# Six-layer stack on Trainium2: key blocks of values copied from the tile's own buffer in 14 or 16 transfers, instead of by a store and a reload through memory off the chip

## The chip, the cores and the metric

One core of one Trainium2 chip runs the whole program. The metric is device time in microseconds (us), from three timed runs and one profiled execution. Smaller is better.

## The reference

The program computes a network of four pairs of blocks (attention over a context, then a feed-forward block). The change touches only the second half of the third pair, a stack of six local-attention layers over x of 2 x 512 tokens x 128. Cut to what matters:

```python
DIM, DEPTH, HEADS, DIM_HEAD, WINDOW = 128, 6, 16, 64, 32     # INNER = 16 * 64 = 1024

def local_attention(q, k, v):                 # each b, h, n, d
    nw = n // WINDOW
    bq, bk, bv = (t.reshape(b, h, nw, WINDOW, d) for t in (q, k, v))
    def look(t):                              # a window's keys: the window before it, and itself
        p = jnp.pad(t, ((0, 0), (0, 0), (1, 0), (0, 0), (0, 0)))
        return jnp.concatenate([p[:, :, :nw], p[:, :, 1:]], axis=3)
    bk2, bv2 = look(bk), look(bv)
    sim = jnp.einsum('bhwie,bhwje->bhwij', bq, bk2) * 8.0
    sim = jnp.where(mask, -big, sim)
    return jnp.einsum('bhwij,bhwje->bhwie', jax.nn.softmax(sim, -1), bv2)

for i in range(DEPTH):
    x = attn_layer(shift_tokens(x), Wqkv[i], q_scale[i], k_scale[i], Wo[i]) + x
    x = ffn_layer(shift_tokens(x), ln_g[i], ln_b[i], W1[i], b1[i], W2[i], b2[i]) + x
```

Each window of 32 queries mixes 64 values: those of the window before it and its own. `look` is the step whose values are moved here.

## The kernel before

The program is written by hand, engine by engine, with semaphores; nothing schedules it. `Stack` (line 1208 on) cuts the six layers into N = 48 tiles of 128 tokens, four to a unit (one batch element of one layer), two units to a layer. Tile T is number t = T % 4 of its unit. The loops of PE (TensorE), ACT (ScalarE) and DVE (VectorE) run over T and work on several tiles at once: in the pass of T they project tile T + 2, turn queries and keys of T + 1, score and mix T and add T - 1. SyncE runs `sp_shift(T)` for T = 0 to 47 and, behind it, the loads of the next layer's weights: one of three `wqkv` parts after tiles 3, 4 and 5 of a layer (`load_w`), five more transfers after tile 6 (`load_f`).

The path of the values:

- `act_proj`, line 1397: ACT copies tile T's values (128 tokens x 1,024) from PSUM into `v[:, t % 2, :]`, in two halves. There are two such buffers, so tile T takes the one of tile T - 2.
- `sp_shift`, line 1329: SyncE stores the tile's values to `st_v_out`, 512 KB, in memory off the chip, and signals `v_stored`.
- `v_load`, line 1319: it loads them back into `vv` in another order. `vv` holds for each of four windows w of a tile, in four partition ranges of 32 rows, the keys of half e of the heads, h = 1 for the window itself and h = 0 for the one before. Even and odd tiles have their own four places. A tile's loads: 32 x 4 x 512 (h = 1) and 32 x 3 x 512 (h = 0, windows 1 to 3) for each e, and, where t > 0, two of 32 x 512 from the tile before for window 0. For t = 0 window 0 has no window before it, and its place keeps what is masked away.
- `pe_mix`, line 1586: PE multiplies with `vv`, waits for `vshift[t]` and `p_evac`, and signals `pv_done`. `sp_shift(T)` waits for `pv_done` of tile T - 2 before it writes `vv` again.

The lines of the chain's view in this stretch: 1385 projections, 1404 squares, 1420, 1428 and 1433 rotations and sums, 1493 turns of queries and keys, 1514 scores, 1566 turns of probabilities, 1575 their copy `pT`, 1610 turns of the output, 1619 their copy `oT`, 1634 output projection, 1657 and 1670 of the layer norm.

## Time and profile before

| | us |
|---|---|
| median of 3 timed runs | 1956.83 (1955.41 to 1961.53) |
| the profiled execution's own time | 1947.39 |
| its span, first to last instruction | 1945.5 |
| of it the stack, about 563 to 1466 | 903 |

PE is busy in 83% of the span, DVE in 65%, ACT in 50%, POOL in 39%. A busy share is a sum over all stages. What ends a wait in one stage stands in the list of waits (engine and line, what it waited for, total, times, longest) and in the chain, which is followed back from the last instruction. SPq is SyncE's queue: its rows are transfers being issued, and the time from issue to landing stands in the list of DMA issues.

### The profile page before, as it was taken

To read this page: it belongs to the slowest core of one execution; us is meant where nothing else is said; L and a number is where in the kernel's file an instruction comes from. 1 tells how busy PE (TensorE), PEld (TensorE's weight loads), DVE (VectorE), ACT (ScalarE), POOL (GpSimd) and SP (SyncE) were. 2 spreads that over 40 slices of the span, in tenths; PEclk is the share of its full clock that TensorE was granted. 3 is DMA by queue.
4 is the path that set the end of the run, shared out by engine and by line. 5 is a ranking of instruction groups with operands and counts; after the bars stand their busy time and mean duration, and the time that the engine had idled before them with its cause. 6 is when DMAs were issued, how large, how long until landed. Compare 5 with 4: busy or idle time off the path is not lost.

```text
span 1945.5 us, 42200 instructions
## 1 busy us (share of the span) xinstructions
PE 1621.7 (83%) x17249; PEld 1097.3 (56%) x17249; DVE 1255.0 (65%) x2361; ACT 968.0 (50%) x1729; POOL 761.1 (39%) x1082
## 2 busy tenths in 40 slices
PE   3005576999767899989999889999987999999999
PEld 1002254676545666656666656666663677667576
DVE  6847684212866788868888778888853666666311
ACT  1034133332235567656666566666654666666332
POOL 0000020100247666766776657766740333334000
PEclk7556798899888999999999999999998999999999
DMA  3000002010033343433433343343311000000111
GB/s 108 20 4 0 3 1 62 22 33 14 1 113 98 98 117 102 124 81 105 118 103 102 101 102 101 117 109 89 96 35 43 2 1 1 1 2 1 33 33 33
DMA packets 73661, 113.33 MB, mean 58 GB/s; under 512 B 15942, under 2 KB 36012, under 8 KB 73438
## 3 DMA queue, kind: packets, MB, share of 16 engines
q1 hardware_dynamic: 72654, 110.40, 20.6%
q8 instruction: 138, 2.26, 0.5%
q14 instruction: 53, 0.43, 0.1%
q10 hardware_dynamic: 816, 0.24, 0.1%
HBM read 83.95 MB, written 27.50 MB: 57 GB/s over the span
## 4 chain that ended last, share of the span: by engine, by line
PE 60%; DVE 27%; issue 6%; ACT 4%; DVEq 1%; DMA 1%; POOL 0%; ACTq 0%; POOLq 0%; SPq 0%
PE PS L1385 7%; PE PS L1115 6%; PE PS L1106 6%; PE PS L2089 4%; PE PS L2043 3%; PE PS L1634 3%; PE PS L2068 3%; DVE st_t L1428 3%; DVE st_ss L1433 3%; PE PS L1514 2%; DVE st_r L1420 2%; PE PS L1493 2%; PE PS L1586 2%; PE PS L1733 2%; DVE al_hist L459 2%
## 5 line engine op out<-in xcount | busy, mean ns | idle before, releaser
L1462 POOL TENSOR_TENSOR st_r<-st_r,st_t 128x512 f32<-128x512 f32 x192 | 243.6, 1274 | 205.8 <-DVE st_t L1428 205.8
L1385 PE MATMUL PS<-st_wqkv,st_xs 128*128 128x512 f32 x576 | 304.8, 614 | 12.5 <-DVE st_t L1428 8.0
L2174 POOL TENSOR_SCALAR la_p<-la_p,la_rden 128x589 f32<-128x589 f32 x64 | 112.7, 1761 | 245.8 <-DVE la_rden L2193 245.8
L1479 POOL TENSOR_TENSOR st_r<-st_r,st_gy 128x512 f32<-128x512 f32 x192 | 195.1, 1047 | 3.8
L1420 DVE TENSOR_TENSOR st_r<-PS,st_rot 128x512 f32<-128x512 f32 x192 | 129.3, 673 | 99.0 <-ACT st_sqh L1404 98.4
L2187 DVE TENSOR_REDUCE la_nmx<-PS 128x1 f32<-128x589 f32 x128 | 92.7, 766 | 91.8 <-PE PS L2051 91.8
L2149 ACT ACTIVATE la_p<-PS,la_nmx 128x589 f32<-128x589 f32 x128 | 95.0, 747 | 106.6 <-DVE la_nmx L2187 106.6
L1174 ACT ACTIVATE m_h<-PS 128x512 f32<-128x512 f32 x128 | 76.1, 597 | 140.8 <-PE PS L1106 140.8
L1404 ACT ACTIVATE st_sqh<-PS 128x512 f32<-128x512 f32 x192 | 114.4, 596 | 57.4 <-PE PS L1385 56.3
L1199 DVE SCALAR_TENSOR_TENSOR m_y<-PS,m_g,m_y 128x128 f32<-128x128 f32 x112 | 31.5, 345 | 161.0 <-PE PS L1115 161.0
L1428 DVE TENSOR_TENSOR st_t<-PS,st_rot 128x512 f32<-128x512 f32 x192 | 130.6, 680 | 0.0
L1115 PEld LDWEIGHTS PS<-m_w,m_h 128*128 128x128 f32 x1024 | 121.4, 196 | 16.0 <-issue 16.0
L800 POOL MEMSET l_s<- 128x144 f32 x2 | 0.4, 220 | 330.9 <-DVE x L643 216.7
L1433 DVE TENSOR_REDUCE st_ss<-st_sqh 128x8 f32<-128x512 f32 x192 | 129.8, 676 | 0.0
L1493 PEld LDWEIGHTS PS<-cst,st_r 128*128 128x128 f32 x768 | 91.2, 144 | 62.7 <-issue 45.0
L1115 PE MATMUL PS<-m_w,m_h 128*128 128x128 f32 x1024 | 121.7, 279 | 3.0 <-DVE m_y L1201 3.0
L1106 PE MATMUL PS<-xn,m_w 128*128 128x512 f32 x256 | 116.3, 600 | 0.0
L1634 PEld LDWEIGHTS PS<-st_oT,st_wo 128*128 128x128 f32 x768 | 94.7, 200 | 38.0 <-ACT st_oT L1619 29.2
L1493 PE MATMUL PS<-cst,st_r 128*128 128x128 f32 x768 | 111.1, 278 | 4.5 <-POOL st_r L1479 3.7
L1634 PE MATMUL PS<-st_oT,st_wo 128*128 128x128 f32 x768 | 102.9, 289 | 4.8 <-issue 2.7
L1385 PEld LDWEIGHTS PS<-st_wqkv,st_xs 128*128 128x128 f32 x576 | 89.5, 195 | 27.1 <-DVE st_t L1428 16.4
L1514 PEld LDWEIGHTS PS<-st_kT,st_qT 64*32 64x32 f32 x6144 | 64.6, 105 | 62.3 <-issue 62.3
(313 smaller groups left out, 3487.4 us busy)
## 6 DMA issues: line engine op xcount, KB each, us to landing
st_v_out<-st_v SPq DMA_DIRECT2D x48, 512.0 KB, 2.6
st_vv<-st_v_out SPq DMA_DIRECT2D x96, 256.0 KB, 4.2
st_vv<-st_v_out SPq DMA_DIRECT2D x96, 192.0 KB, 4.5
st_wqkv<-in_st_wqkv SPq DMA_DIRECT2D x18, 512.0 KB, 5.7
m_w<-in_m_w SPq DMA_DIRECT2D x32, 256.0 KB, 3.1
st_vv<-st_v_out SPq DMA_DIRECT2D x72, 64.0 KB, 1.9
st_wo<-in_st_wo SPq DMA_DIRECT2D x6, 512.0 KB
st_w<-in_st_w SPq DMA_DIRECT2D x6, 341.0 KB
```

The costliest lines, as they stand in the source:

```text
L1106: pe.matmul(PS[:, c, :], self.w1[:, e % 2, P * c:P * c + P], xn[:, b, :], start=True, stop=True)\
L1115: mm = pe.matmul(PS[:, 4 + u % 2, P * j:P * j + P], self.h[:, u % 2, c, P * j:P * j + P], self.w2[:, e % 2, c, :], start=(c == 0), stop=(c ...
L1385: pe.matmul(PS[:, 2 + m % 2, :], self.xs[:, b, P * t:P * t + P], self.wqkv[:, l % 2, k, 512 * half:512 * half + 512], start=True, stop=Tru ...
L1404: act.activation(self.sqh[:, c % 2, :], ps, ACT.Square).then_inc(self.squares, 1)
L1420: dve.tensor_tensor(h3(self.r[:, t % 2, c, :]), h3(ps), self.rot[:, k, 0, t, :].unsqueeze(1) .broadcast_to([P, 8, D2]), ALU.mult)
L1428: dve.tensor_tensor(h4(self.t2[:, c % 2, :]), turned, self.rot[:, k, 1, t, :] .rearrange("p (s d) -> p s d", s=2).unsqueeze(1).broadcast_t ...
L1433: dve.tensor_reduce(self.ss[:, t % 2, 8 * c:8 * c + 8], h3(self.sqh[:, c % 2, :]), X, ALU.add)\
L1462: pool.tensor_tensor(r, r, self.t2[:, c % 2, :], ALU.add).then_inc(self.added, 1)
L1479: pool.tensor_tensor(r, r, y[:, 8 * c:8 * c + 8].unsqueeze(2).broadcast_to([P, 8, D2]), ALU.mult)\
L1493: mm = pe.transpose(PS[:, 4 + g % 2, P * j:P * j + P], self.r[:, T % 2, g, P * j:P * j + P], ident)
L1634: mm = pe.matmul(PS[:, 7, 0:P], self.wo[:, l % 2, c, :], self.oT[:, c, :], start=(c == 0), stop=(c == 7))
L2174: pool.tensor_scalar(self.p[:, v % 2, 0, :], self.p[:, v % 2, 0, :], self.rden[:, v % 4, 0:1], None, ALU.mult).then_inc(self.scaled0, 1)
```

## The change

`st_v_out`, its store and the wait for it are gone. `v_copy` copies a block of 32 rows x 512 values from `v` straight into its place in `vv`, one transfer for each window w, half e and h: 14 for t = 0 and 16 for the others. The two copies for window 0 from the tile before come first and signal a semaphore of their own, one for even and one for odd tiles (`v_crossed`; the odd one is `al_costs_out`, used earlier in the program and left at 64). The other 14 signal `vshift[t]`. ACT, before it overwrites `v[t % 2]`, waits for the 14 copies of tile T - 2 and the crossed pair of tile T - 1, instead of the store of T - 2. PE waits for the crossed pair too where t > 0.

```diff
-            self.v_out = dram("st_v_out", (4, P, INNER))
...
-        def v_load(self, sp, T, e, h, first, count, to, signal):
+        COSTS_OUT = 64
+        OWN, CROSS = (8 + 6) * 16, 2 * 16
+
+        def v_copy(self, sp, T, e, h, w, signal):
 
+            source = 4 * T + w - (1 - h)
             rows = slice(64 * e + WIN * h, 64 * e + WIN * h + WIN)
-            src = view(self.v_out, ((T % 4) * P + WIN * first) * INNER + 512 * e,
-                       [[INNER, WIN], [WIN * INNER, count], [1, 512]])
-            sp.dma_start(self.vv[rows, to:to + count, e, :], src).then_inc(self.vshift[signal], 16)
+            block = slice(WIN * (source % 4), WIN * (source % 4) + WIN)
+            sp.dma_start(self.vv[rows, 4 * (T % 2) + w, e, :],
+                         self.v[block, source // 4 % 2, 512 * e:512 * e + 512]).then_inc(signal, 16)
+
+        def crossed(self, T):
+
+            odd, units, t = T % 2, T // self.TILES, T % self.TILES
+            count = 2 * units + (t + 1) // 2 if odd else units + t // 2
+            return self.v_crossed[odd], (0, self.COSTS_OUT)[odd] + count * self.CROSS
 
         def sp_shift(self, sp, T):
 
             t = T % self.TILES
-            at = 4 * (T % 2)
-
             sp.wait_ge(self.v_evac, T * 2 + 2)
-            if T >= 4:
-                sp.wait_ge(self.pv_done, T - 3)
-            sp.dma_start(self.v_out[t], self.v[:, t % 2, :]).then_inc(self.v_stored, 16)
-
             if T >= 2:
                 sp.wait_ge(self.pv_done, T - 1)
             if t > 0:
                 for e in range(2):
-                    self.v_load(sp, T - 1, e, 0, 3, 1, at, t)
-            sp.wait_ge(self.v_stored, T * 16 + 16)
+                    self.v_copy(sp, T, e, 0, 0, self.v_crossed[T % 2])
             for e in range(2):
-                self.v_load(sp, T, e, 1, 0, 4, at, t)
-                self.v_load(sp, T, e, 0, 0, 3, at + 1, t)
+                for w in range(4):
+                    self.v_copy(sp, T, e, 1, w, self.vshift[t])
+                    if w:
+                        self.v_copy(sp, T, e, 0, w, self.vshift[t])
...
                 if m == 0 and T >= 2:
 
-                    act.wait_ge(self.v_stored, T * 16 - 16)
+                    act.wait_ge(self.vshift[(T - 2) % self.TILES], ((T - 2) // self.TILES + 1) * self.OWN)
+                    act.wait_ge(*self.crossed(T - 1))
...
             pe.wait_ge(self.p_evac, 2 * T + 2)
-            pe.wait_ge(self.vshift[t], (u + 1) * (64 if t == 0 else 96))
+            pe.wait_ge(self.vshift[t], (u + 1) * self.OWN)
+            if t:
+                pe.wait_ge(*self.crossed(T))
```

SyncE, tile 2 of the first layer, before: `v_out` is the tensor off the chip, `vv` the mixing's buffer.

```order
L1329 DMA st_v_out<-st_v 128x1024 [waits st_v_evac]
L1319 DMA st_vv<-st_v_out 32x512 [waits st_pv_done]
L1319 DMA st_vv<-st_v_out 32x512
L1319 DMA st_vv<-st_v_out 32x4x512 [waits st_v_stored]
L1319 DMA st_vv<-st_v_out 32x3x512
L1319 DMA st_vv<-st_v_out 32x4x512
L1319 DMA st_vv<-st_v_out 32x3x512
```

SyncE, tiles 2 to 4 of the first layer, after, with the weight loads that stand behind tile 3.

```order
L1325 DMA st_vv<-st_v 32x512 [waits st_pv_done,st_v_evac]
L1325 DMA st_vv<-st_v 32x512 x15
L1325 DMA st_vv<-st_v 32x512 [waits st_pv_done,st_v_evac]
L1325 DMA st_vv<-st_v 32x512 x15
L1292 DMA st_qks<-in_st_qks 128x256 [waits st_rot_ready]
L1297 DMA st_wqkv<-in_st_wqkv 128x1024
L1325 DMA st_vv<-st_v 32x512 [waits st_pv_done,st_v_evac]
L1325 DMA st_vv<-st_v 32x512 x13
```

Seven issues with three places to wait became sixteen with one, and the weight loads stand behind a longer row.

ACT, the pass of tile 2, before: the copy into `v` stands between the two copies of `oT`.

```order
L1619 ACTIVATE st_oT<-PS 128x512 [waits st_wo_done,st_o_turned]
L1397 ACTIVATE st_v<-PS 128x512 [waits st_v_stored,st_proj]
L1619 ACTIVATE st_oT<-PS 128x512 [waits st_o_turned]
L1397 ACTIVATE st_v<-PS 128x512 [waits st_proj]
L1549 ACTIVATE st_e<-st_e 128x1024 [waits st_sub_done]
```

The same place after.

```order
L1630 ACTIVATE st_oT<-PS 128x512 [waits st_wo_done,st_o_turned]
L1406 ACTIVATE st_v<-PS 128x512 [waits al_costs_out,st_vshift2,st_proj]
L1630 ACTIVATE st_oT<-PS 128x512 [waits st_o_turned]
L1406 ACTIVATE st_v<-PS 128x512 [waits st_proj]
L1558 ACTIVATE st_e<-st_e 128x1024 [waits st_sub_done]
```

Nothing moved in ACT's row; the first copy into `v` waits for the copies of two tiles in place of one store.

PE, the mixing of tile 2, before.

```order
L1493 MATMUL PS<-cst,st_r 128x128 [waits st_p_evac,st_r_ready]
L1493 MATMUL PS<-cst,st_r 128x128 x3
L1586 MATMUL PS<-st_vv,st_pT 32x128 [waits st_vshift2,st_p_evac]
L1586 MATMUL PS<-st_vv,st_pT 32x128 x31
L1493 MATMUL PS<-cst,st_r 128x128 [waits st_p_evac,st_r_ready]
```

The same place after.

```order
L1502 MATMUL PS<-cst,st_r 128x128 [waits st_p_evac,st_r_ready]
L1502 MATMUL PS<-cst,st_r 128x128 x3
L1597 MATMUL PS<-st_vv,st_pT 32x128 [waits st_v_crossed_even,st_vshift2,st_p_evac]
L1597 MATMUL PS<-st_vv,st_pT 32x128 x31
L1502 MATMUL PS<-cst,st_r 128x128 [waits st_p_evac,st_r_ready]
```

One name more is waited for ahead of the same matmul.

## Rows read from the trace of the kernel before

**Rows 1.** Page, busy time and chain, whole span.
```profile
PE 1621.7 (83%) x17249; PEld 1097.3 (56%) x17249; DVE 1255.0 (65%) x2361; ACT 968.0 (50%) x1729; POOL 761.1 (39%) x1082
...
PE 60%; DVE 27%; issue 6%; ACT 4%; DVEq 1%; DMA 1%; POOL 0%; ACTq 0%; POOLq 0%; SPq 0%
```

**Rows 2.** Stack's stretch: us; busy PE, PEld, DVE, ACT, POOL; PEclk, DMA, GB/s.
```profile
563.00:1466.00 903.00, 830.12 (x12466) 555.00 (x12466) 706.63 (x1092) 570.00 (x931) 597.03 (x985) 0.98 0.37 101
```

**Rows 3.** Waits of SyncE's queue, whole span: total us, times, longest.
```profile
SPq L1329 <- ACT st_v L1397: 376.6, 48, 12.8
...
SPq L1319 <- PE PS L1586: 288.2, 46, 11.5
...
SPq L1336 <- DMA st_v_out<-st_v: 25.0, 11, 2.3
```

**Rows 4.** One line's view: mixing L1586 (idle until), then L1397 (idle until).
```profile
L1586 PE MATMUL PS<-st_vv,st_pT x3072: 272/273/298, 600.3 to 1453.8; 128*32 128x128 f32 x192
...
  issue: 6.7, 40
  ACT st_pT L1575: 2.9, 9
...
  PE PS L1385: 53.7, 53
```

**Rows 5.** Issues, ns min/median/max; then the list of transfers, us to landing.
```profile
L1319 SPq DMA_DIRECT2D st_vv<-st_v_out x264: 303/429/1279, 574.2 to 1424.2; - x132
L1329 SPq DMA_DIRECT2D st_v_out<-st_v x48: 326/338/342, 570.1 to 1413.6; - x48
...
st_vv<-st_v_out SPq DMA_DIRECT2D x96, 192.0 KB, 4.5
...
st_vv<-st_v_out SPq DMA_DIRECT2D x72, 64.0 KB, 1.9
```

**Rows 6.** Timeline (start, us): SyncE's batches, ACT's copies into `v`, one mixing.
```profile
660.98 2.69 SPq L1319 DMA_DIRECT2D st_vv<-st_v_out  x6
...
666.10 0.60 ACT L1397 ACTIVATE st_v<-PS 128x512 f32<-128x512 f32 x1
...
937.08 1.75 SPq L1319 DMA_DIRECT2D st_vv<-st_v_out  x4
...
952.25 2.68 SPq L1319 DMA_DIRECT2D st_vv<-st_v_out  x6
...
957.32 0.60 ACT L1397 ACTIVATE st_v<-PS 128x512 f32<-128x512 f32 x1
...
965.89 1.95 PE L1586 MATMUL PS<-st_vv,st_pT 128*32 128x128 f32 x64
...
967.91 2.84 SPq L1319 DMA_DIRECT2D st_vv<-st_v_out  x6
...
1388.25 3.52 SPq L1319 DMA_DIRECT2D st_vv<-st_v_out  x6
...
1393.32 0.60 ACT L1397 ACTIVATE st_v<-PS 128x512 f32<-128x512 f32 x1
```

**Rows 7.** Timeline, copies with both ends on the chip, and who waited.
```profile
20.08 6.70 SPq L305 DMA_DIRECT2D al_skew<-al_dist  x8
...
27.92 1.63 ACTq L305 DMA_DIRECT2D al_skew<-al_dist  x2
...
32.36 0.01 DVE L454 LOAD_MASK_SELECT al_hist<-al_hist  x1 [2.42 <-DMA al_skew<-al_dist]
```

**Rows 8.** Waits of PE in the stack; then the timeline's longest of them.
```profile
PE PS L1514 <- issue: 22.7, 9, 4.2
...
630.38 0.22 PEld L1514 LDWEIGHTS PS<-st_kT,st_qT 64*32 64x32 f32 x12 [4.32 <-issue]
```

**Rows 9.** Page, DMA queue and kind: packets, MB, share of 16 engines.
```profile
q8 instruction: 138, 2.26, 0.5%
...
HBM read 83.95 MB, written 27.50 MB: 57 GB/s over the span
```

## Prediction before the changed kernel was run

> **What bounds the kernel now.** I read the page's busy shares and its chain first [rows 1]: TensorE is busy for 83% of the span and carries 60% of the chain, VectorE 27%, DMA 1%. So an edit that touches only transfers can pay only where a transfer ends a wait. All of it lies in the six-layer stack, 563 to 1466 us, where the table by stretch shows PE busy 830 of 903 us at a granted clock of 0.98 (all but the full 2.4 GHz level) and the transfer engines at a 0.37 share [rows 2]. Next the waits of the DMA queue [rows 3]: SyncE's two longest in the stack are for ACT's copies of the values (376.6 us) and for PE's mixing (288.2 us). SyncE waits for the compute; on its own store it waits 25.0 us, in 11 places. The reader should then see who waits for what SyncE delivers: L1586, the mixing that reads `vv`, sat idle 6.7 us for "issue" and 2.9 us for ACT's `pT`, and names no DMA at all; L1397, ACT's copy into `v`, waits for PE alone (53.7 us) and for no store [rows 4]. The round trip through memory is wholly hidden.
>
> **Part 1, the store and its wait go.** 48 stores of 0.34 us issue, and SyncE's waits for them [rows 3, 5]. Nobody on the chain stood behind either: 0 us. What is late next is what was late already, the release by the mixing two tiles earlier, since both kernels may write `vv` only then.
>
> **Part 2, 4 or 6 loads become 14 or 16 copies, all on SyncE's queue.** A batch is released when a mixing ends and must be issued before the next. In the old batch the six issues take 2.68 us together, 0.45 each with their gaps, and the 64 KB ones are no cheaper behind another than the 256 KB ones (median of all 0.43) [rows 5, 6]. I take this pace, because shape, queue and neighbours are the same as in the new copies (32 rows of 2 KB): 16 x 0.45 = 7.1 us and 14 x 0.45 = 6.3 us. What the trace of before does not show is a copy of this shape with both ends on the chip. The nearest are the skewed rows: eight issued in 6.70 us, 0.84 each [rows 7]; with them a batch takes 13.4 us. Below, 0.31 (the first issue of a batch can be as short as 0.303 [rows 5]) would give 5 us. None of the ends changes the time: mixings start every 18.15 us in the mean (48 from 600.3 to 1453.6 [rows 4]), and in the tightest stretch SyncE is released at 937.1, 952.2 and 967.9 us, so 15.2 and 15.7 us apart [rows 6]. Even 13.4 us with one weight load behind it (0.45 by the same pace) fits; the five loads behind tile 6 add 2.3 us, 15.7 in all at the dear end, to a batch that has about the mean. What is queued behind the batches is these weight loads for the next layer, 4 us later than now (at 0.84 some 9 us), and not needed before that layer begins, over two tiles on. **Price: 0 us**; from both sides -0 to +0.
>
> **Part 3, the new waits.** (a) PE before the mixing now waits for `vshift` and a crossed pair. The order shows that the third condition sits with the others before the same matmul, and no instruction is added. The copies of a batch land 7.1 + 1.9 = 9 us after release; the mixing that reads them comes two mixings later, at the least 28.8 us on (937.1 to 965.9 [rows 6]). Slack 20 us; with 0.84 us issues and the slowest landing below still 12. (b) ACT before `v` of tile T+1 must have the own copies of T-1 and the crossed pair of T. This is the only tight place. Own copies: SyncE released at 937.1, ACT writes at 957.32 [rows 6]: 20.2 us for 6.3 + 1.9 = 8.2 us, or 11.8 + 3.6 = 15.4 at the dear ends. Crossed pair: released at 952.2, ACT writes at 957.32, so 5.1 us; the same 5.1 stands at 660.9 to 666.1 and at 1388.2 to 1393.3 [rows 6], eleven tiles in all (each second tile of a unit from T = 5 to 45); the other tiles, by the same reading, have more. Before, ACT waited there only for the store of the tile before. The pair needs 0.06 to start, 0.31 + 0.02 for the first issue and 1.9 from the second issue to landing [rows 5]: 2.3 us, 2.8 to spare. The landing of on-chip copies is bounded by the skewed rows: the last two are issued from 27.92 for 1.63 us, so the last from about 28.7, and VectorE goes on at 32.36 [rows 7]: at most 3.6 us. Dear end: 0.06 + 0.84 + 3.6 = 4.5 us, still under 5.1. I take the cheap value, since size and shape are those of the 64 KB loads. Behind the waiting ACT stand the second `oT` copy and the exponentials, so PE's L1634 and then the chain would be held. At both ends of the sum: **0 us**.
>
> The Trainium skill, DMA: Bandwidth & Descriptors, section Rules for kernel authors, speaks against this change: many small transfers should be joined into one, as under 64 KB one pays mostly overhead, and its section on the anatomy of a DMA gives a fixed cost near 2 us. The 1.9 us to landing of the 64 KB loads [rows 5] agree with such a cost; by the row it is paid beside the next issue, by the rule read strictly one after another, which is the serial rival below.
>
> **Part 4, traffic.** Per tile 512 KB stored and up to 1,024 KB loaded become up to 1,024 KB copied: 524 KB per 18.15 us is 29 of the 101 GB/s [rows 2], so by bytes the share should fall from 0.37 to about 0.26. Does anybody gain? PE stands still for a reason that the profile doesn't name: 22.7 us in 9 places before L1514, the longest 4.2 to 4.3 us, at a burst of short matmuls [rows 8]. Queue q8 brings 138 pieces of instructions, 2.26 MB, at 0.5% of 16 engines' span, so 0.005 x 16 x 1945.5 / 138 = 1.13 us each [rows 9]. If these pauses are waits for code, each holds one such piece, and less traffic may shorten it, or a batch that lasts longer (9 us; now 0.45 x 5 + 4.5 to landing = 6.8 [rows 5]) may meet it more often. At a fourth of 1.13 us nine pauses change by 2.5 us, at a half by 5, either sign. PE's program keeps its length, so the pauses stay where they are. I take 0 with +-4.
>
> The Trainium skill, Runtime: NRT & Kernel Launch, section Instruction fetch mechanics, has code come in blocks of 256 instructions and mostly hidden; by that this term would be nothing, and the row with 4.3 us speaks against "hidden" for PE's bursts.
>
> **Sum.** 0 + 0 + 0 + 0 (+-4) us on the profiled execution's 1947.39 (span 1945.5). The median of the timed runs, 1956.83, lies 9.4 us above; I carry that over unchanged and round: 1957 us.
>
> **Rivals.** (1) *SyncE becomes the bound* (slower). If an on-chip copy holds the queue for what the longest load did, 1.279 us [rows 5], eight tiles need 124 copies x 1.279 + 9 other issues x 0.45 = 162.6 us where the compute needs 8 x 18.15 = 145.2. That is +17.4 us per eight tiles, +100 us over 46 tiles: 2057 us. It decides from (145.2 - 4) / 124 = 1.14 us a copy. For it: the skewed rows are already twice as dear as loads. Against: these write one partition from 77, the new ones 32 rows from 32, and the store, whose source is on the chip, is issued in 0.34. 5%. (2) *ACT is held by the crossed pair* (slower): if on-chip pairs land after 6.5 us instead of 2.3, the eleven tight tiles lose 1.4 us each, +15 us, 1972. It decides from 5.1 us after release. 5%. (3) *Serial copies*: each waits for the one before, 15.5 x 1.9 = 29.5 us a tile against 18.15, +11.3 x 46 = +520 us, 2477. Against: the two 64 KB loads, issued 0.4 us apart, have the same 1.9 us median. 1%. (4) *More pauses of PE* by meeting traffic, over 0.65 us in each of nine: +6 to +10 us, 1965. 3%. (5) *Fewer pauses* or weights that land sooner: -6 to -10 us, 1949. 6%. (6) The change doesn't do what it says: bytes written to memory don't fall; then also nothing moves. Under 1%, since the order shows the store gone.
>
> **How the numbers follow.** The forecast of no change has 80%. Within 0.3% (5.9 us, about what a measurement can tell from no change): 0.80; slower 0.14 (rivals 1 to 4); faster 0.06. The range is +-4 us of part 4 with the scatter of the runs of before around their median (-1.4 to +4.7), and reaches toward rivals 4 and 5: 1949 to 1967. Rivals 1 and 3 are left out.
>
> **What would show it.** In the profile after: no L1329 row; 744 copies, back-to-back issues of 0.43 us and a batch of about 7 us; landings near 1.9 us all through the batch, as a copy gives each engine 4 KB per 0.43 us; written bytes down from 27.5 by 25 MB to about 2 MB; ACT's L1406 (old L1397) naming no DMA as releaser, and the pause of PE before the mixing still 6.7 us. SyncE released again 15.2 and 15.7 us apart at the place of [rows 6]. The forecast fails if copies are issued at over 1.14 us, if SyncE is never seen waiting for the mixing, or if ACT waits for `vv<-v` in the second tile of a unit.

## The result, and the profile after

The kernel after takes 1941.31 us (median of 17 runs, 1934.58 to 1953.83) where the kernel before, run beside it, takes 1956.83 (17 runs, 1944.31 to 1965.02): 15.5 us less, ratio 0.9922 with a 95% interval of 0.9905 to 0.9939. The prediction was 1957.0 with a range of 1949 to 1967, so it was wrong: the time is below the range, on the side of rival 5, and about one and a half to two and a half times as far as that rival went.

First the page of the kernel after: busy time, transfers, chain. The rows of before are [rows 1] and [rows 9].

```profile
PE 1627.3 (84%) x17249; PEld 1100.9 (57%) x17249; DVE 1254.2 (65%) x2361; ACT 968.1 (50%) x1729; POOL 761.9 (39%) x1082
...
q1 hardware_dynamic: 73422, 85.26, 16.9%
q8 instruction: 138, 2.26, 0.5%
...
HBM read 35.19 MB, written 2.34 MB: 19 GB/s over the span
...
PE 59%; DVE 28%; issue 6%; ACT 4%; DVEq 1%; DMA 1%; POOL 0%; ACTq 0%; POOLq 0%; SPq 0%
```

The reader sees that the change did what it says (25.2 MB less written, 48.8 MB less read), and that shares and chain look as before. Nothing in these rows tells of a gain. The stack's stretch of the kernel after (columns as in [rows 2]):

```profile
563.00:1466.00 903.00, 838.82 (x12479) 559.12 (x12477) 709.36 (x1096) 571.72 (x934) 600.06 (x985) 0.98 0.29 74
```

The granted clock is the same 0.98, the transfers' share fell from 0.37 to 0.29, and PE is busy 8.7 us more in the same 903 us: it stands still less. Then the views of single lines of the kernel after: the copies (issue time in ns, min/median/max), the mixing that reads them, and ACT's copy of the values, each with what ended its engine's idle time. The old numbers of these lines are L1319, L1586 and L1397.

```profile
L1325 SPq DMA_DIRECT2D st_vv<-st_v x744: 507/591/2004, 572.5 to 1421.4; - x186
```

```profile
L1597 PE MATMUL PS<-st_vv,st_pT x3072: 272/273/297, 602.7 to 1443.5; 128*32 128x128 f32 x192
...
  issue: 6.2, 37
  ACT st_pT L1584: 3.4, 12
```

```profile
L1406 ACT ACTIVATE st_v<-PS x96: 587/597/603, 570.3 to 1402.8; 128x512 f32<-128x512 f32 x96
...
  PE PS L1393: 53.6, 61
```

Neither the mixing nor ACT's copy names a transfer, just as in [rows 4]: the new waits cost nothing. But from the first matmul of the first mixing to the last matmul of the 48th it is now 840.8 us (602.7 to 1443.5) where it was 853.5 [rows 4]. That is 12.7 us, and more than the 6.1 us by which the two profiled spans differ (1945.5 and 1939.4): in this execution the first mixing starts 2.4 us later and what follows the last is 4.2 us longer. The 12.7 us are found in the waits of PE between 560 and 1470 us. After (us in total, times, longest; before [rows 8]: 22.7, 9, 4.2):

```profile
PE PS L1523 <- issue: 15.2, 7, 2.9
...
PE PS L1621 <- issue: 3.3, 2, 2.0
...
PE PS L1645 <- issue: 0.5, 1, 0.5
```

The other two in before stood at the turn of `on` and the projection behind it:

```profile
PE PS L1610 <- issue: 6.5, 2, 3.5
...
PE PS L1634 <- issue: 2.7, 2, 1.8
```

Together 31.9 us before and 19.0 after, a difference of 12.9: the whole of it. Tile by tile, read from the two traces, the distance from one mixing to the next is the same to 0.2 us in 28 of 47 tiles (15.2, 15.7, 18.0 and 21.2 us, by the place in the unit), and the 19 others lie within three tiles of such a pause in one kernel or the other. So everything that follows is about these pauses, "idle until issue", in which PE waits for nothing that the profile names.

One rival is the clock. In six of the eleven pauses over 0.9 us of the kernel before, the granted clock falls from the full level (2.4 GHz) to the lower one (1.2 GHz) within the pause or at most 1.2 us behind it, for 3.4 or 6.8 us; for example behind the pause of 4.0 us at tile 28 (columns as in [rows 2]):

```profile
1128.90:1132.30 3.40, 3.40 (x12) 2.33 (x11) 2.14 (x2) 2.05 (x3) 3.40 (x4) 0.51 0.03 7
```

From this mixing to the next it is 24.1 us instead of 18.0, more than the pause alone. Over the whole stack it hardly counts between these two executions, though: from the first mixing to the last PE is busy 795.8 us before and 795.2 after. The difference is idle time.

**What the pauses are.** PE's records of one execution are 17,249 matmuls and 17,249 weight loads (page) and 849 waits and the like, 35,347 in all, and q8 brings 138 pieces: 256.1 instructions to a piece. Counted along the stream, every pause over 0.9 us in the stack stands at the same place of a block, at instruction 193 or 194 of 256, in every kernel below, also in those whose stream is shifted. In all of them PE goes on 1.2 to 1.6 us after a piece of q8 has landed. Each time PE passes such a place (from here on, a crossing) one piece starts on q8, nearly always behind it. In each pause PE stands at the next crossing until this piece is there, so it holds what comes after that next crossing. And why there: the scores of a tile are 128 matmuls with 128 weight loads, so 256 instructions in some 1.4 us, while a whole tile, about 532 of them (2,127 to a unit of four tiles, waits included), takes 18. Every burst of scores meets a block boundary, and where two crossings come close together in time and the piece of the earlier one is late, PE runs dry. The longest pause of before, row by row. The timeline of before (start, duration; the end of the pause is the row at 630.38 in [rows 8]):

```profile
620.86 1.84 SPq L1319 DMA_DIRECT2D st_vv<-st_v_out  x4
...
622.75 0.43 SPq L1292 DMA_DIRECT2D st_qks<-in_st_qks  x1
...
623.22 0.43 SPq L1297 DMA_DIRECT2D st_wqkv<-in_st_wqkv  x1
...
624.82 1.24 PEld L1514 LDWEIGHTS PS<-st_kT,st_qT 64*32 64x32 f32 x116 [1.47 <-issue]
```

Transfers of before in 626 to 629 us: busy tenths in 40 slices, then queue, packets, MB, share of 16 engines.

```profile
DMA  9899997988996969796989875319010000000000
...
q1 hardware_dynamic: 268, 0.64, 66.6%
q8 instruction: 1, 0.02, 2.3%
```

PE got through 116 of the 128 weight loads and stopped at 626.06. It had passed the crossing before this one at 621.5. The queue of the data, q1, works at 60% or more of the engines to 627.8 and is done at 628.2 (66.6% is the mean of the whole window); the one piece of q8 runs from 628.08 to 629.18 by the trace, 6.6 us behind the crossing and just as that traffic ends, and PE goes on at 630.38. The same place in the kernel after, timeline and then transfers in 628 to 629.5 us:

```profile
622.08 11.41 SPq L1325 DMA_DIRECT2D st_vv<-st_v  x16
...
626.82 1.40 PEld L1523 LDWEIGHTS PS<-st_kT,st_qT 64*32 64x32 f32 x116 [1.47 <-issue]
...
630.47 0.22 PEld L1523 LDWEIGHTS PS<-st_kT,st_qT 64*32 64x32 f32 x12 [2.25 <-issue]
```

```profile
q1 hardware_dynamic: 104, 0.13, 35.9%
q8 instruction: 1, 0.02, 4.5%
```

Same instruction, 116 and 12 on either side of it, but 2.25 us instead of 4.32. The piece runs from 628.12 to 629.21, 4.6 us behind its crossing, with copies in flight at 35.9%. It takes 1.1 us as before; what changed is how late it starts. The two weight transfers, 128 and 512 KB, are out of the way too: with 16 issues ahead of them they start at 633.5.

The Trainium skill, Runtime: NRT & Kernel Launch, section Instruction fetch mechanics, says that code comes in 16 KiB blocks of 256 instructions, which the 256.1 instructions and 16.4 KB (2.26 MB / 138) per piece bear out, and that crossing a block's boundary is mostly hidden. For PE's bursts here it is not: 31.9 us of this stack.

### The profile page after: what moved, and what is told of

It is laid out like the page before. It is cut to its first block, busy times and chain, and to the rows that moved or that the text cites. A ratio compares the mean times of both kernels' runs of the same rounds, so it can differ in the third digit from the quotient of the medians.

```text
span 1939.4 us, 42623 instructions
## 1 busy us (share of the span) xinstructions
PE 1627.3 (84%) x17249; PEld 1100.9 (57%) x17249; DVE 1254.2 (65%) x2361; ACT 968.1 (50%) x1729; POOL 761.9 (39%) x1082
## 3 DMA queue, kind: packets, MB, share of 16 engines
q8 instruction: 138, 2.26, 0.5%
## 4 chain that ended last, share of the span: by engine, by line
PE 59%; DVE 28%; issue 6%; ACT 4%; DVEq 1%; DMA 1%; POOL 0%; ACTq 0%; POOLq 0%; SPq 0%
PE PS L1393 7%; PE PS L1115 6%; PE PS L1106 6%; PE PS L2100 4%; PE PS L1645 4%; DVE st_t L1437 4%; PE PS L2054 3%; PE PS L1523 3%; PE PS L2079 3%; DVE st_r L1429 3%; DVE st_ss L1442 3%; DVE st_den L1562 2%; PE PS L1744 2%; DVE al_hist L459 2%; PE PS L1502 1%
## 5 line engine op out<-in xcount | busy, mean ns | idle before, releaser
L1393 PE MATMUL PS<-st_wqkv,st_xs 128*128 128x512 f32 x576 | 302.9, 610 | 13.3 <-DVE st_t L1437 8.6
L1523 PEld LDWEIGHTS PS<-st_kT,st_qT 64*32 64x32 f32 x6144 | 69.0, 105 | 54.6 <-issue 53.7
```

The source lines that it names most:

```text
L1393: pe.matmul(PS[:, 2 + m % 2, :], self.xs[:, b, P * t:P * t + P], self.wqkv[:, l % 2, k, 512 * half:512 * half + 512], start=True, stop=Tru ...
L1523: mm = pe.matmul(PS[WIN * w:WIN * w + WIN, e, D2 * c:D2 * c + D2], self.qT[64 * e:64 * e + 64, c, WIN * w:WIN * w + WIN], self.kT[64 * e:6 ...
```

## The experiments

All ratios are to the kernel before, run in turn on the same chip, with 95% intervals. "Mixings" is the time from the first mixing's first matmul to the last one's last (before 853.5, after 840.8 us); "pauses" the sum of PE's pauses over 0.9 us in the stack that end with issue, counted from the trace (before 30.4 us in 11 places, after 18.4 in 9). Both come from one profiled execution of each kernel, the ratios from all its runs. Of each edit the lines that matter are shown; the changed counts of the waits that follow from it are left out. **Theory A**: large transfers in flight hold back the pieces of q8. Its first rival, theory B in the expectations of the first round: the round trip itself (store, bytes of memory off the chip) did. **Theory C** stands there for "not the values' traffic at all"; in section 5 it is this: how many pauses there are is set by where the block boundaries fall.

**1. Which part of the change gains: four kernels.** split64 is before with its large loads cut to 64 KB and the store kept:

```
-                self.v_load(sp, T, e, 1, 0, 4, at, t)
-                self.v_load(sp, T, e, 0, 0, 3, at + 1, t)
+                for w in range(4):
+                    self.v_load(sp, T, e, 1, w, 1, at + w, t)
+                    if w:
+                        self.v_load(sp, T, e, 0, w - 1, 1, at + w, t)
```

> The kernel before, with its store kept and its 4 or 6 loads cut into 14 or 16 loads of 64 KB from memory, as many as the changed kernel has copies. In the traces of both kernels the mixings follow each other at equal distances wherever TensorE does not stand still without a named releaser ('issue'); the changed kernel has 18.4 us of such pauses over 0.9 us in the stack where the one before has 30.4. Theory A (TensorE waits there for a block of code, whose transfer comes late behind a burst of large loads): the burst is spread out here, so pauses fall to about 20 us and the time to about -8 us or more (0.995). Theory B (it is the bytes from and to memory off the chip that delay the code, which comes from there too): as before, within 3 us. Theory C (the difference of the two kernels is not in the values' traffic at all): as before.

nostore is before with the store only in the first four tiles, so later tiles load old values:

```
-            sp.dma_start(self.v_out[t], self.v[:, t % 2, :]).then_inc(self.v_stored, 16)
+            if T < 4:
+                sp.dma_start(self.v_out[t], self.v[:, t % 2, :]).then_inc(self.v_stored, 16)
```

> The kernel before, with its large loads kept, but the store made for the first four tiles alone: later tiles load the values of the first four again, so this is not the reference's computation; only the store (24 MB) is left out. Theory A: the burst behind the mixing stays, so pauses stay near 30 us and the time within 3 us of before, or a little less. Theory B: a third of the bytes is gone, and all writes, pauses about 25 us, -5 us. Theory C: as before.

split64_nostore has both edits:

> As the run without the store (values of the first four tiles loaded again, not the reference's computation), and the loads cut into 14 or 16 of 64 KB. It differs from the changed kernel only in that the source is memory off the chip. Theory A: like the changed kernel, -12 to -16 us (0.992), pauses 18 to 20 us. Theory B: between the two, about -6 us. Theory C: as before.

after_store is after with the store put back, ahead of the copies:

```
+            for k in range(1):
+                sp.dma_start(self.v_out[t, k], self.v[:, t % 2, :]).then_inc(self.v_stored, 16)
```

> The changed kernel, with the store of each tile's values put back where it was (SyncE issues it first, ACT waits for it before it overwrites v; nothing reads what is stored). Theory A: small effect, the store stands 5 to 8 us ahead of the burst: within 4 us of the changed kernel. Theory B: half of the gain is lost, about -8 us to before. Theory C: like the changed kernel.

| kernel | loads or copies | store | ratio | mixings | pauses |
|---|---|---|---|---|---|
| nostore | 2 x 256, 2 x 192 KB | no | 1.0029 (1.0011 to 1.0047) | 853.3 | 31.2 |
| split64 | 14 x 64 KB from memory | yes | 0.9923 (0.9902 to 0.9944) | 836.6 | 16.5 |
| split64_nostore | 14 x 64 KB from memory | no | 0.9930 (0.9906 to 0.9954) | 839.9 | 18.7 |
| after | 14 x 64 KB on the chip | no | 0.9922 (0.9905 to 0.9939) | 840.8 | 18.4 |
| after_store | 14 x 64 KB on the chip | yes | 0.9935 (0.9912 to 0.9958) | 838.2 | 18.7 |

This is a clean factorisation. To leave out the store gains nothing (with large loads it even costs 0.3%), and neither does it matter where the data come from: the four kernels with 64 KB lie within each other's intervals. The cut to 64 KB is worth the whole gain at this position of the block boundaries (section 5). split64 moves as many bytes off the chip as before (read 83.95, written 27.50 MB) at nearly the same share of the transfer engines:

```profile
563.00:1466.00 903.00, 837.13 (x12485) 555.04 (x12486) 710.65 (x1099) 574.57 (x939) 597.79 (x985) 0.98 0.35 101
```

0.35 at 101 GB/s against 0.37 at 101 [rows 2], and yet as fast as after at 0.29 and 74. So neither bytes nor the mean share explain the gain; how the transfers are cut does. Cutting changes two things at once, the size of one transfer and how far a batch is spread out in time (six issues in 2.7 us [rows 6] against 16 in 7 to 9 in the trace of split64), and no run here takes them apart.

**2. Put large transfers back.** after_burst2 adds two stores of 512 KB behind the crossed pair of every tile:

```
+            sp.wait_ge(self.v_stored, 256 + T * 32)
+            for k in range(2):
+                sp.dma_start(self.v_out[t, k], self.v[:, t % 2, :]).then_inc(self.v_stored, 16)
```

> The changed kernel, and behind each tile's crossed pair two stores of the tile's 512 KB to memory that nobody reads, so that 1 MB of large transfers stands behind each mixing again, where the large loads of the kernel before stood. Theory A (a block of code for TensorE comes late behind a burst of large transfers): the pauses come back at the same tiles (0 to 3, 12 to 14, 26 to 28), 28 us or more in sum instead of 18, and the gain of 15 us is lost, 0 +-5 us to the kernel before; ACT is not held (its copies have 20 us). Theory B (the gain is that values no longer come from memory): the loads stay away, most of the gain stays, -10 us.

Measured 0.9930 (0.9909 to 0.9951), mixings 843.5, pauses 20.4 us. A miss for theory A as I had put it: 50 MB more are written, the stack's stretch has a share of 0.43 at 130 GB/s, more than the kernel before (0.37 at 101), and the pauses did not come back. Two stand where after has none (2.9 us at tile 16, where a piece came 6.1 us late just behind a mixing, and 2.7 us at tile 28), and one of after's, 2.9 us at tile 43, is gone. (after_split_w, below, has a pause of 2.8 us at tile 16 too, and split64_nostore one of 2.2 us at tile 28, without these stores.) Large *stores* do little. So the next kernel put back what before really had, large *loads*, 32 rows high, into a buffer that nobody reads:

```
+            for e in range(2):
+                for h in range(2):
+                    rows = slice(64 * e + WIN * h, 64 * e + WIN * h + WIN)
+                    src = view(self.v_out, (t * P) * INNER + 512 * e,
+                               [[INNER, WIN], [WIN * INNER, 3 + h], [1, 512]])
+                    sp.dma_start(self.spare[rows, 0:3 + h, :], src).then_inc(self.v_stored, 16)
```

> The kernel after, with four large loads per tile put back from memory off the chip (two of 256 KB, two of 192 KB, all 32 rows high, into a buffer that nobody reads) between the crossed pair and the 14 own copies; nobody but the next tile's loads waits for them. Theory A (large loads in flight hold back the instruction blocks that TensorE is sent on queue q8, and the pauses of 2 to 4 us in front of the scores and the turns come from that): the pauses of the stack come back from 18 us in all to 26 to 31, at tiles 0 to 3 and 26 to 28 above all, and the time to 1950 to 1957, ratio 0.997 to 1.000. Theory B (the size of single transfers does not matter, it is what waits for the large loads that gained): ratio stays 0.990 to 0.995 and the sum of pauses below 21 us.

Measured 1.0035 (1.0007 to 1.0063), above the 0.997 to 1.000 of theory A: the gain is gone and a little more. Mixings 864.3 us, pauses 34.1 us in 13 places. Waits of PE, then two lines of its timeline at the place shown above:

```profile
PE PS L1541 <- issue: 26.9, 10, 3.9
...
PE PS L1639 <- issue: 5.5, 2, 3.0
```

```profile
628.09 1.74 SPq L1358 DMA_DIRECT2D st_spare<-st_v_out  x4
...
634.05 0.21 PEld L1541 LDWEIGHTS PS<-st_kT,st_qT 64*32 64x32 f32 x12 [4.05 <-issue]
```

Four large loads issued at 628.09, the burst of scores behind them, and the pause is 4.05 us again, with all 16 copies there and no round trip for the values; only the next tile's dummy loads wait for these four. (In the first four tiles a store of 512 KB fills what they load, and ACT waits for it.) The piece of q8 runs here from 631.37 to 632.56, in the middle of the loads' traffic: it is late, but it need not wait for their end. (Here the traffic is also more, 123 GB/s, so this run by itself doesn't tell bytes from size; split64 does.)

Then the dose. split128 cuts the large loads only in half:

```
+                for w in (0, 2):
+                    self.v_load(sp, T, e, 1, w, 2, at + w, t)
+                self.v_load(sp, T, e, 0, 0, 1, at + 1, t)
+                self.v_load(sp, T, e, 0, 1, 2, at + 2, t)
```

> The kernel before with its four large loads cut in half only: eight loads of 64 or 128 KB where split64 had fourteen of 64 KB; store kept. Theory A (size of a transfer sets how late a block of instructions comes): half-way, pauses of 20 to 27 us in all, ratio 0.994 to 0.998. Rival (what matters is that the loads are spread out by SyncE's 0.4 us an issue rather than their size): eight issues spread them over 3.5 us instead of 6, also about half-way, so this run tells dose from threshold and not these two apart. Rival C (any cut does it, by chance of the phase): 0.992.

0.9943 (0.9915 to 0.9971). The middle of it lies between the two, as theory A says, but the interval holds split64's 0.9923, so a dose isn't shown. The profiled execution was one of its slower ones (1954.18, median 1947.33) with pauses of 28.7 us.

**3. No traffic of the values at all.** no_copies leaves the 16 copies and their waits out, so the mixings read a buffer that is never filled:

> The changed kernel without its copies and the waits for them: the mixing reads the zeros that were set once, so this is not the reference's computation. It shows what of the pauses remains without any traffic of values. Theory A: the pauses that stay are those whose code is asked for in the burst of short matmuls itself, 14 to 18 us; the time is 0 to 5 us below the changed kernel. If traffic of values had nothing to do with them: 18 us and the changed kernel's time.

0.9948 (0.9926 to 0.9970), pauses 24.8 us in 13 places, among them tiles 30, 31, 41, 42 and 44, where no kernel so far had one. I had expected the floor and got more pauses. The run was confounded: with the wait gone PE's stream is one instruction per tile shorter, 48 in all, and the boundaries slide along. A useful miss, since it was the first sign that their place counts. no_copies_same leaves the same copies and their waits out, but keeps a wait that is always met in front of each mixing:

```
+            pe.wait_ge(align.costs_out, 64)
```

> The kernel after without the 16 copies of a tile (the mixings read a buffer that is never filled, so this part of the computation is left out), and with one wait that is always met in front of each mixing, so that TensorE's stream of instructions is as long as in the other kernels and its blocks of 256 begin at the same places. Theory A: with no values' traffic at all the pauses that remain are those whose delay has another cause; at most those of the kernel after: 10 to 18 us in all, ratio 0.988 to 0.992. Rival (pauses do not depend on the traffic of the values): 18 to 25 us, 0.992 to 0.995.

0.9875 (0.9839 to 0.9910), pauses 16.4 us in 9 places, at the same tiles as after. So, by one execution of each, 16 of the pauses' 30 us have nothing to do with the values' transfers; after, with its 18.4, has already taken most of what is to be had from them.

**4. Large weight loads too?** after_split_w cuts the weight loads of layers 1 to 5 in four:

```
+            for i in range(0, P, n):
+                sp.dma_start(self.wqkv[i:i + n, l % 2, k, :], src[i:i + n]).then_inc(self.w_in, 16)
```

> The changed kernel with the weight loads of layers 1 to 5 cut as well: the 512 KB and 341 KB loads into four of 32 partitions each (nine transfers a layer become 24). Theory A: the pauses at tiles 12 to 14, just behind the weight loads of tiles 11 to 14, and at 26 to 28 shrink by 1 to 3 us in sum; 0 to -4 us to the changed kernel. If weight loads have no part in it: like the changed kernel, unless SyncE's longer row (11 issues behind the 16 copies, some 15 us) holds the next crossed pair: then up to +5 us.

0.9931 (0.9906 to 0.9956), pauses 18.9 us: no gain over after.

**5. Move the boundaries and nothing else.** Forty turns of a constant more on PE ahead of the stack make its stream 80 instructions longer:

```
+            for k in range(40):
+                pe.transpose(PS[:, 5, 0:P], ident, ident)
```

> The changed kernel with 40 turns of a constant block on TensorE ahead of the stack, while it waits there for VectorE: its instruction stream is 80 instructions further on from there. In both traces each pause over 0.9 us that names no releaser and is no wait for ACT's table stands at an instruction whose place in TensorE's stream is 193 or 194 modulo 256, and a unit of four tiles is 2127 = 8 x 256 + 79 instructions long. Theory A (a pause is a wait for the next block of 256 instructions): the clusters of pauses at tiles 12 to 14 and 26 to 28 move four tiles ahead, to 8 to 10 and 22 to 24, and the one at 40 to 36; the sum stays within 5 us. If the pauses belong to the tile (its weight loads, say): they stay at 12 to 14 and 26 to 28.

> The kernel before, large loads and store kept, with the same 40 turns more on TensorE ahead of the stack that took the kernel after to 0.990. If only the places of the block boundaries decide: the same gain as there, 0.990, with pauses of about 10 us. If place and large loads both count (theory A): the boundaries meet other bursts, the crossings shortly behind a mixing are still answered 4 to 7 us late, and the pauses come to 15 to 25 us, ratio 0.993 to 0.998.

after_shift80: 0.9904 (0.9871 to 0.9938, from three runs of 1930.79 to 1936.64 us; a fourth took 5577.72 us, for a reason that nothing here shows, and is left out), pauses 10.3 us in 6 places; those of tiles 0 to 3 are gone, and the others stand at tiles 9, 10, 22 to 24 and 36, four tiles earlier than they were, as the expectation had worked out from blocks of 256. before_shift80, with large loads and store: 0.9892 (0.9861 to 0.9922), pauses 14.6 us in 6. The kernel *before* becomes at least as fast as the kernel after by 40 needless turns, 80 instructions. The burst at tile 1, before_shift80's timeline: 128 weight loads in one piece, where [rows 8] has the stop after 116.

```profile
626.75 1.34 PEld L1514 LDWEIGHTS PS<-st_kT,st_qT 64*32 64x32 f32 x128 [1.47 <-issue]
```

Here the clock has a share: from the first mixing to the last PE is busy 790.8 us where it was 795.8 in before, 5 of the 19 us by which the mixings are closer together. That left open whose the gain was, and four more kernels asked it, both at this position again and at a third (80 turns, 160 instructions), on one chip:

> The kernel before with the 40 turns more, once again, now beside its partner with copies on the same chip. Theory C (what the change is worth depends on where the block boundaries of TensorE's stream fall): before_shift80 keeps its 0.989 and the partner is not faster by more than 0.3%. Theory A alone (large loads always cost about 0.7%): the partner is faster by 0.5 to 1%.

> The kernel after with the 40 turns more, again, beside its partner with large loads. Theory C: 0.985 to 0.990, level with or at most 0.4% ahead of the partner. Theory A alone: 0.98 to 0.984.

> The kernel before with 80 turns more ahead of the stack (160 instructions of TensorE's stream): a third position of the block boundaries. Theory C: pauses anywhere from 10 to 35 us, at tiles other than those of before; so a time from 0.985 to 1.005 with nothing else changed. If the position mattered only by the accident of one place: within 0.3% of before.

> The kernel after with the same 80 turns more. Pauses stand at the same tiles as in before_shift160 and are each as long or shorter by 1 to 3 us where the block is asked for within some 6 us behind a mixing. Theory C: ahead of before_shift160 by 0 to 1%, in proportion to the pauses that fall behind a mixing there; theory A alone: by 0.6 to 0.9%.

| stream longer by | large loads, store | 64 KB copies | mixings | pauses |
|---|---|---|---|---|
| 0 | 1 | 0.9922 | 853.5 / 840.8 | 30.4 / 18.4 |
| 80 (second time) | 0.9914 (0.9887 to 0.9940) | 0.9893 (0.9864 to 0.9921) | 834.3 / 833.7 | 15.6 / 13.3 |
| 160 | 0.9950 (0.9928 to 0.9971) | 0.9927 (0.9900 to 0.9954) | 844.6 / 828.2 | 20.3 / 10.7 |

In each row of this table the kernel with copies is ahead. By the ratios it is 0.8%, 0.2% and 0.2%, the last two within the intervals; by the medians 15.5 us (0.8%), 5.7 (0.3%: five runs of 1932.70 to 1940.15 against five of 1937.57 to 1940.73) and 7.5 (0.4%: six of 1934.71 to 1947.04 against twelve of 1942.73 to 1958.29). In the first round at 80, on two different chips, it was not ahead (0.9904 and 0.9892). (With 160 the mixings say 16.4 us, but that profile of before_shift160, at 1958.29 us, is the slowest of its 12 runs; by the medians, 1948.2 and 1940.7, it is 7.5 us. The added turns themselves put the first mixing off, from 600.3 to 605 to 608 us with 40 of them and to 610 to 612 with 80.) Moving the boundaries alone is worth 1.1% and 0.9% (two measurements) and 0.5% to the kernel before. Theory A alone, which asked for 0.98 to 0.984 in after_shift80_b, is out; both count.

**Both mechanisms in one table.** For 98 boundaries of the stack, the time from PE's crossing of a boundary to the start of its piece on q8, in us, counted from the traces: the mean over those that PE crosses 0.5 to 7 us behind a mixing, that is, while a batch of values is in flight (37 to 41 of them), and over the others.

| kernel | behind a mixing | elsewhere |
|---|---|---|
| before | 2.29 | 1.26 |
| nostore | 2.37 | 1.30 |
| after_burst_loads | 2.48 | 1.46 |
| split128 | 2.03 | 1.41 |
| split64 | 1.47 | 1.44 |
| after | 1.30 | 1.46 |
| after_burst2 (large stores) | 1.74 | 1.50 |
| no_copies_same | 1.41 | 1.39 |
| before_shift80, again | 1.93, 1.86 | 1.24, 1.16 |
| after_shift80, again | 1.38, 1.18 | 1.29, 1.38 |
| before_shift160 | 1.98 | 1.42 |
| after_shift160 | 1.53 | 1.59 |

The left column is 1.9 to 2.5 with large loads and 1.2 to 1.5 with 64 KB transfers at all three positions, about the 1.4 of no copies at all; the right one doesn't follow the loads. This is theory A. The large stores lie between, at 1.74. But a late piece costs time only where PE uses up the block it has before the piece is there, and that is a matter of position. Three single boundaries (us from crossing to piece, then the pause that follows where there is one):

| crossed | before | nostore | burst_loads | split64 | after | no copies, same |
|---|---|---|---|---|---|---|
| tile 1, 1.5 us behind the mixing | 6.6, 4.2 | 6.8, 4.5 | 6.0, 3.9 | 4.8, 2.5 | 4.6, 2.1 | 4.6, 2.2 |
| tile 3, 0.9 us behind | 5.5, 2.6 | 7.0, 3.8 | 4.0, 1.3 | -0.5 | -0.5 | -0.5 |
| tile 28, 3 us behind | 6.4, 4.0 | 6.9, 4.5 | 5.2, 3.1 | 0.9 | 0.3 | 1.4 |

(Below zero: the piece was under way before the crossing.) In the kernel before, the two weight transfers stand close behind the loads of tile 1, so that first row is not the values' loads alone; after_burst_loads has the pause without them. The first row also shows what I can't explain: 4.6 us with no values' traffic whatever. Nine such pieces, 4.6 to 7.0 us late, are left in the kernel after, and at the same boundaries in the kernel without copies.

## Why the prediction was wrong, point by point

- **What bounds the kernel**: right. It read PE as the bound, and the round trip as hidden. nostore (1.0029) shows that nothing is gained by leaving out the store and its wait.
- **Part 1, the store goes: 0**. Right, by nostore and by after against after_store (0.9922 and 0.9935).
- **Part 2, the copies on SyncE's queue: 0**. Right in the result, off in the pace: the median issue is 0.59 us, not 0.43, and a batch takes 9.5 us for 14 copies and 11.0 for 16, 0.68 and 0.69 each, between my cheap end (16 x 0.45, which is 7.2 us and not the 7.1 that I wrote) and my dear 13.4. I took the pace of the loads because shape and queue were the same; the source on the chip was what differed, and the skewed rows [rows 7], which had that, were the nearer ones (0.84). split64 shows it, with the same 744 transfers of 64 KB from memory in a median of 0.42 us:

```profile
L1319 SPq DMA_DIRECT2D st_vv<-st_v_out x744: 302/421/2020, 575.9 to 1413.2; - x186
```

The bounds held. At the dear end the weight loads would have been 10.7 us later (13.4 less 2.7) and not "some 9", which changes nothing either. Rival 1 (from 1.14 us a copy) and rival 3 (serial copies) didn't come. SyncE still waits for the mixings, now longer than in [rows 3]:

```profile
SPq L1339 <- PE PS L1597: 313.0, 46, 12.9
```

- **Part 3, new waits: 0**. Right. The copies land in 2.0 us (1.9 to 3.7, the longest 0.1 over my bound of 3.6). The tight place came as the order had it: in the timeline of after the batch starts at 945.16 and ACT writes `v` at 950.18, 5.0 us later (predicted 5.1), with no idle time in its row. Batches are released 15.2 us apart, as foreseen.

```profile
930.00 9.51 SPq L1325 DMA_DIRECT2D st_vv<-st_v  x14
...
945.16 11.02 SPq L1325 DMA_DIRECT2D st_vv<-st_v  x16
...
950.18 0.60 ACT L1406 ACTIVATE st_v<-PS 128x512 f32<-128x512 f32 x1
```

- **Part 4, traffic: 0 +-4. This is the step that failed.** It saw the right place, nine pauses of 22.7 us before the scores, and guessed their nature, waits for code. It then priced them by the piece: 1.13 us each, to be changed by a fourth or a half of that, so at most 5 us over nine. But a pause is not the piece's own transfer; it is how late that piece is *begun*. The longest pause, 4.2 us, was already four times the 1.13, and that contradiction stood in its own sentences. By the traces the piece at tile 1 comes 6.6 us after the crossing with large loads and 4.6 with small copies, a pause shrinks by 2.1 us (4.32 to 2.25) or vanishes whole (4.0 us at tile 28, 2.6 at tile 3), and the sum is -12.9 us on the profiled execution. The piece itself takes 1.1 us before and after, so the term that was priced did not change at all.
- "PE's program keeps its length, so the pauses stay where they are" was right, and more important than I made of it: it is the reason that the two kernels can be compared at all, and why no_copies could not. What I didn't see is that the same pauses at another place, as after 80 more instructions, would have made another price: the 15.5 us are for this position, 5.7 and 7.5 for the two others.
- **The bytes were the wrong handle.** Part 4 argued with the share of the transfer engines (0.37 to 0.26; measured 0.29). split64 leaves bytes and share nearly as they are and has the whole gain. The edit that matters was filed under part 2, as a cost in issues, and never as a change of transfer size.
- **9.4 us from the profiled execution to the median** were carried over unchanged. The fall of the medians is 15.5 us and that of the mixings 12.7; the profiled execution of before (1947.39) was among its faster ones, and the remaining 3 us are within what separates single runs.
- **Rival 5** (fewer pauses, -6 to -10 us, 6%) is what happened, at -15.5. It should have been priced by the pauses' length. By hindsight: if a fourth to a half of 31.9 us go, that is -8 to -16 us, and the range should have reached to 1941 at least.

The Trainium skill, DMA: Bandwidth & Descriptors, section Rules for kernel authors, would join small transfers into large ones. The prediction weighed that rule only for what it might cost in serial time. Here the opposite edit, with bytes, source and store unchanged, ran at 0.9923: what a large transfer saves in issues on an idle queue it cost in the start of the pieces on another queue.

## What to carry to other kernels

When a bound engine has pauses that end with "issue", count its instructions: where the pauses stood at the same place in every 256, as here, it waited for code, and the price was how late the piece was begun (up to 7.6 us), not how long it took (1.1 us). Transfers that nobody waits for can still set that: try the same bytes in smaller transfers, spread out, before removing any. And before a gain of under 1% in such a kernel is put down to an edit, shift the program by some tens of instructions with and without it; here the shift alone was worth as much as the edit (0.989 to 0.995 against 0.992), and what the edit was worth went from 0.8% to 0.2 to 0.4%.

## What was not expected of the hardware

- PE's pauses sit at instruction 193 or 194 of a block of 256, and PE goes on 1.2 to 1.6 us after the piece has landed; in the kernel before they take 31.9 us of a stretch in which PE is otherwise the bound.
- Pieces of q8 start 1.2 to 1.6 us behind a crossing in the mean, 1.9 to 2.5 us where loads of 128 to 256 KB are in flight, and 4 to 8 us at single places. Two 512 KB stores per tile had a smaller effect (1.74 us; 20.4 us of pauses against 18.4), four loads of 192 and 256 KB brought it back (2.48 us; 34.1). Why loads and not stores is open: the two kernels also differ in the height of the transfer (32 rows against 128) and in where the bytes go, which wasn't taken apart.
- Pieces that come 4 to 8 us late with no value in flight still leave 16.4 us of pauses without the copies. Their cause is open.
- A copy of 64 KB with both ends on the chip, 32 rows of 2 KB each, is issued in a median of 0.59 us against 0.42 for the same rows from memory (split64), and lands in 2.0 us in both.
- In the kernel before the granted clock fell to 1.2 GHz for 3.4 or 6.8 us at six of the eleven pauses.
